# Weight tiles ahead of x in the set-up, a reordered start of the second phase, one image summed by TensorE, and the last chunk finished in thirds

## What is computed

```python
def _attn_kernel(x, w1, b1, w2, b2, bn_gamma, bn_beta, bn_mean, bn_var):
    k = lax.conv_general_dilated(x, w1, (1, 1), padding=[(PAD, PAD), (PAD, PAD)], rhs_dilation=(DIL, DIL), ...)
    k = jax.nn.relu(k + b1[None, :, None, None])          # 128 channels, 7x7, dilation 2
    k = lax.conv_general_dilated(k, w2, (1, 1), 'VALID', ...) + b2[None, :, None, None]   # 49 taps
    ...                                                   # batch norm, relu
    return jax.nn.softmax(k, axis=1)
x = x + conv_ref(_ln_c(x))        # conv_ref: sum over 49 taps of shifted x * attention[tap]
t = _to_tokens(x)
# ffn(_ln_t(t)): one routing per batch element from the mean over its tokens, top 2 of 8 experts,
# gelu(x @ W1 + b1) @ W2 + b2 weighted by the routing, + x, layer norm with gamma and beta
t = t + ffn(_ln_t(t), ...)
```

## Time and profile before

| | us |
|---|---|
| median of 3 runs | 1017.62 |
| lowest and highest of them | 1015.72, 1018.93 |
| profiled execution, its time | 1019.93 |
| profiled execution, its span | 1018.1 |
| TensorE busy (matrix products) | 928.7 |
| VectorE busy | 733.8 |
| ScalarE busy | 544.9 |
| GpSimd busy | 146.2 |

### The profile page before, as it was taken

One profiled execution on the slowest core, in us unless ns is written; L12 is line 12 of the kernel. 1 busy time (PEld: TensorE's weight loads), 2 busy tenths in 40 slices (PEclk: granted clock), 3 DMA queues, 4 the chain that ended last, 5 costly groups with the idle time before them and its releaser, 6 DMA issues. The chain is left out here.

```text
span 1018.1 us, 18938 instructions
## 1 busy us (share of the span) xinstructions
PE 928.7 (91%) x7375; PEld 708.9 (70%) x7375; DVE 733.8 (72%) x1820; ACT 544.9 (54%) x985; POOL 146.2 (14%) x163
## 2 busy tenths in 40 slices
PE   2678999999999999979999925999999999999997
PEld 1567666776677667646999913777777777777776
DVE  4776456559637844977579864778987897888876
ACT  5677333435443512223555435768768686686851
POOL 1100001000100011100213220111111121112111
PEclk9999999999999999989999967999999999999999
DMA  9722121004101104453458444273345435424311
GB/s 234 192 76 65 31 63 47 25 1 131 52 24 27 59 28 137 149 168 86 123 157 229 122 128 97 60 174 79 63 102 135 93 74 140 108 55 95 63 33 47
DMA packets 135080, 96.02 MB, mean 94 GB/s; under 512 B 63579, under 2 KB 129516, under 8 KB 134892
## 3 DMA queue, kind: packets, MB, share of 16 engines
q1 hardware_dynamic: 134990, 94.81, 36.5%
HBM read 55.95 MB, written 29.40 MB: 84 GB/s over the span
## 5 line engine op out<-in xcount | busy, mean ns | idle before, releaser
L1279 PE MATMUL pM<-V,U 128*128 128x368 f16 (+3 forms) x2016 | 321.0, 315 | 0.0
L1279 PEld LDWEIGHTS pM<-V,U 128*128 128x128 f16 x2016 | 194.9, 98 | 101.6 <-issue 0.8
L2047 PE MATMUL pH<-xT,w1h 128*128 128x384 f16 x768 | 190.7, 331 | 15.2 <-DMA xT<-xs 12.8
L1945 DVE SCALAR_TENSOR_TENSOR gl<-gf,sc,gh 128x384 f16<-128x384 f32 x192 | 145.2, 791 | 58.0 <-ACT gh L1761 57.9
L1770 ACT ACTIVATE gf<-pH,b1c,sc 128x384 f32<-128x384 f32 x192 | 127.7, 669 | 97.8 <-issue 72.8
L2063 PE MATMUL pY<-w2h,gh 128*128 128x256 f16 x576 | 157.0, 273 | 0.0
L2063 PE MATMUL pY<-w2h,gl 128*128 128x256 f16 x576 | 157.0, 273 | 0.0
L2063 PE MATMUL pY<-w2l,gh 128*128 128x256 f16 x576 | 157.0, 273 | 0.0
L744 ACT CAST V<-pV 128x384 f16<-128x384 f32 x96 | 45.5, 477 | 155.9 <-PE pV L1250 155.8
L2047 PE MATMUL pH<-xT,w1l 128*128 128x384 f16 x384 | 126.9, 331 | 0.0
L2047 PEld LDWEIGHTS pH<-xT,w1h 128*128 128x128 f16 x768 | 75.7, 99 | 65.3 <-DMA xT<-xs 12.9
(11 more groups left out here) (251 smaller groups left out, 1321.7 us busy)
## 6 DMA issues: line engine op xcount, KB each, us to landing
xa<-in_xt SPq DMA_DIRECT2D x16, 576.0 KB, 6.5
xs_scratch<-xs SPq DMA_DIRECT2D x16, 576.0 KB, 3.9
tk<-t_scratch SPq DMA_DIRECT2D x24, 384.0 KB, 3.9
out<-o SPq DMA_DIRECT2D x24, 384.0 KB, 2.9
xs<-in_ew SPq DMA_DIRECT2D x16, 512.0 KB, 4.8
U<-xs_scratch SPq DMA_DIRECT2D x16, 480.0 KB, 4.7
w1r<-in_ew SPq DMA_DIRECT2D x8, 512.0 KB, 4.3
w2r<-in_ew SPq DMA_DIRECT2D x8, 512.0 KB, 5.8
```

Of the source, the lines that this page charges most:

```text
L1279: return nc.tensor.matmul(out[:, :, first:end], U[:, k, hi_u, piece, :], V[:, b % 2, hi_v, k, c, :, first + TILES * d:end + TILES * d], st ...
L1945: stt(gl[:, sl, j, :], gf[:, (JB * m + j) % GBUFS, :], scale_of(G_UP), gh[:, sl, j, :], ALU.mult, ALU.subtract).then_inc(g_step, 1)
L2047: last = nc.tensor.matmul(pH[:, (JB * m + j) % HBUFS, 0:CN], w[:, k, c, f * P:(f + 1) * P], xT[:, s, x, c, :], start=(i == 0), stop=(i == ...
```

## The change

It has four parts.

1. **Set-up.** SyncE issues ident, w0 and w1 first, then x0, Gt, Td, x1, the small parameters, x2 and w2 to w7. The data turns of image p lie in pair p, at steps 1 to 6, so image 0's are no longer ahead of pair 0, and pair 3 has six. `x_high`, `x_low` and the normalising of image p + 1 lie in pair p. VectorE runs `spread_mags(0)`, `ln(0)`, `tap_scale(0)`, `ln(1)` ahead of pair 0. The batch-norm steps move to steps 2 and 4 of pair 0.
2. **Image 14.** TensorE sums its tokens (`sum_tokens(14)`) behind the last `attend`; VectorE doesn't accumulate it. The means get one more small reduction.
3. **Start of the second phase.** SyncE waits for the routing right behind the loads of chunks 0 and 1, and issues w1, b1, the transpose of chunk 0, w2, b2, chunk 2, the transpose of chunk 1, beta, gamma, chunk 3, the transpose of chunk 2. ScalarE's and VectorE's `take_x(0, 0)` come earlier, `split_w1(0)` comes ahead of `take_x(0, 1)`, GpSimd's first `add_beta` waits for the split of w1, and b2's sum is a step of its own (`sum_b2`) placed later. `layer1` takes the four products with w1's high half first and waits for the low half only in front of the fifth.
4. **Last chunk.** `finish_last` does sum, statistics, power, scale and end for one tile of 128 tokens after the other, and `store_last` stores each tile by itself.

```diff
@@ -227,9 +227,10 @@
     U_PAIR = PIECES // 2
-    MAGS_FIRST, MAGS_THEN = (1, 4), (1, 3)
+    MAGS_THEN = (1, 3)
+    V_LATE = U_PAIR - V_TURNS
     LN_PARTS, NORM_PARTS = {1: 0, 2: 1, 3: 2}, {0: 0, 2: 1, 4: 2}
-    XHI_AT, SPREAD_AT, BN_AT, LN_BACK_AT = 5, 4, 2, 5
+    XHI_AT, SPREAD_AT, BN_AT, LN_BACK_AT = 5, 4, 4, 5
     XBUFS = 3
@@ -568,20 +569,20 @@
-            load_x(0)
-            sp.dma_start(Td[:, :, :], data_d).then_inc(tab_loaded, 16)
-            load_x(1)
-            sp.dma_start(Gt[:, :], tap_d).then_inc(tap_loaded, 16)
             sp.dma_start(ident[:, :], ident_d).then_inc(id_loaded, 16)
...
                 load_w(sp, g)
-            load_x(2)
-            for g in range(2, OGS):
-                load_w(sp, g)
+            load_x(0)
+            sp.dma_start(Gt[:, :], tap_d).then_inc(tap_loaded, 16)
+            sp.dma_start(Td[:, :, :], data_d).then_inc(tab_loaded, 16)
+            load_x(1)
             sp.dma_start(w2s, w2).then_inc(par_loaded, 16)
...
             sp.dma_start(b1s[:, :], b1).then_inc(par_loaded, 16)
+            load_x(2)
+            for g in range(2, OGS):
+                load_w(sp, g)
             for i in range(BI):
@@ -813,25 +814,22 @@
+            for g in range(2):
+                magnitude(g)
             normalise_x(0)
-            x_high(0)
-            normalise_x(1)
-            for j in range(V_TURNS):
-                v_high(j)
-                if j in MAGS_FIRST:
-                    magnitude(MAGS_FIRST.index(j))
-            x_high(1)
             for pair in range(PAIRS_OG):
...
                     u_high(U_PAIR * pair + j)
-                    if j < V_TURNS and pair + 1 < BI:
-                        v_high(V_TURNS * (pair + 1) + j)
+                    if pair + j == 0:
+                        x_high(0)
+                    if j >= V_LATE:
+                        v_high(V_TURNS * pair + j - V_LATE)
                     if j in MAGS_THEN and pair + 1 < PAIRS_OG:
                         magnitude(2 * (pair + 1) + MAGS_THEN.index(j))
-                    if j in NORM_PARTS and pair + 2 <= BI:
-                        normalise_x(pair + 2, third(NORM_PARTS[j]))
-                    if j == XHI_AT and pair + 2 <= BI:
-                        x_high(pair + 2)
+                    if j in NORM_PARTS:
+                        normalise_x(pair + 1, third(NORM_PARTS[j]))
+                    if j == XHI_AT:
+                        x_high(pair + 1)
@@ -1030,10 +1028,13 @@
+            def added(n):
+                return n - ADDED * BI - (n > BY_PE)
+
             def accumulate(n):
...
                 b, i = n // BI, n % BI
-                s = Steps(dve, acc_step, n - ADDED * BI, NB)
+                s = Steps(dve, acc_step, added(n), NB)
                 s.settle()
@@ -1114,40 +1115,34 @@
+            spread_mags(0)
             ln(0)
+            tap_scale(0)
             ln(1)
-            x_low(0)
-            for j in range(V_TURNS):
-                v_low(j)
-                if j in (1, 3):
-                    ln_stats(2, third(j // 2))
-            spread_mags(0)
-            tap_scale(0)
-            x_low(1)
-            ln(2, third(2))
             for pair in range(PAIRS_OG):
...
                     u_low(U_PAIR * pair + j)
-                    if j < V_TURNS and pair + 1 < BI:
-                        v_low(V_TURNS * (pair + 1) + j)
-                    if j in LN_PARTS and pair + 3 <= BI:
+                    if pair + j == 0:
+                        x_low(0)
+                    if j >= V_LATE:
+                        v_low(V_TURNS * pair + j - V_LATE)
+                    if j in LN_PARTS and pair + 2 <= BI:
                         if LN_PARTS[j] < 2:
-                            ln_stats(pair + 3, third(LN_PARTS[j]))
+                            ln_stats(pair + 2, third(LN_PARTS[j]))
                         else:
-                            ln(pair + 3, third(2))
+                            ln(pair + 2, third(2))
                     if j == SPREAD_AT and pair + 1 < PAIRS_OG:
                         spread_mags(pair + 1)
-                    if pair == 0 and j == 0:
+                    if pair == 0 and j == 2:
                         dve.wait_ge(par_loaded, 16 * 7)
...
                         bn_scales()
-                if pair + 2 <= BI:
-                    x_low(pair + 2)
+                x_low(pair + 1)
@@ -1205,8 +1200,6 @@
                     normalise(B - 1, n - 1)
-                if n == IMGS - 1:
-                    accumulate(n - 1)
                 statistics(n)
@@ -1220,21 +1213,22 @@
             means = mean[:, :].rearrange("p (c b) -> p c b", c=CC)
-            dve.wait_ge(tokens_summed, ADDED * BI + B - ADDED)
+            dve.wait_ge(tokens_summed, ADDED * BI + B - ADDED + 1)
             dve.wait_ge(shifts_summed, B)
...
             nc.vector.tensor_reduce(means[:, :, 0:ADDED], summed[:, :, 0:ADDED], AX.X, ALU.add).then_inc(mean_step, 1)
-            nc.vector.tensor_copy(means[:, :, ADDED:B], summed[:, :, ADDED:B, 0]).then_inc(mean_step, 1)
+            nc.vector.tensor_copy(means[:, :, ADDED:B - 1], summed[:, :, ADDED:B - 1, 0]).then_inc(mean_step, 1)
+            nc.vector.tensor_reduce(means[:, :, B - 1], summed[:, :, B - 1, 0:BI:BY_PE % BI], AX.X, ALU.add).then_inc(mean_step, 1)
             nc.vector.tensor_reduce(shifts, pC[:, SHIFTS:SHIFTS + NB * IMGS].rearrange("p (b x) -> p b x", b=B),
...
             nc.vector.tensor_copy(wsum[:, :], pC[:, SUMS_AT:SUMS_AT + UNITS]).then_inc(wsum_taken, 1)
...
@@ -1337,16 +1331,15 @@
-            pe.wait_ge(tab_loaded, 16)
             pe.wait_ge(set_up, POOL_SET)
-            for j in range(V_TURNS):
-                turn_v(j)
             bound(0)
...
                     turn_u(U_PAIR * pair + j)
-                    if j < V_TURNS and pair + 1 < BI:
-                        turn_v(V_TURNS * (pair + 1) + j)
+                    if pair == 0 and j == V_LATE:
+                        pe.wait_ge(tab_loaded, 16)
+                    if j >= V_LATE:
+                        turn_v(V_TURNS * pair + j - V_LATE)
                     if j == U_PAIR - 2 and pair + 1 < PAIRS_OG:
@@ -1499,6 +1492,7 @@
                     sum_shifts(n // BI - 1)
+            sum_tokens(BY_PE)
             turn_stats(B - 1)
@@ -1645,6 +1642,12 @@
+            def store_last():
+                n = B * CHUNKS - 1
+                for t in range(CT):
+                    sp.wait_ge(end_step, E_ALL * (t + 1))
+                    sp.dma_start(out[ds(n * CN + t * P, P), :], o[:, n % 2, t]).then_inc(out_stored[n % 2], 16)
+
             def load_experts(b):
@@ -1657,6 +1660,8 @@
                     sp.dma_start(b1r[:, k], ew_b(eb1, e)).then_inc(b1_loaded, 16)
+                if is_first(b):
+                    turn_x(0, 0)
                 for k, e in enumerate(chosen):
@@ -1668,13 +1673,15 @@
                 load_chunk(0, m)
+            sp.wait_ge(r_step, 16)
+            load_experts(0)
+            load_chunk(0, 2)
+            turn_x(0, 1)
             sp.dma_start(bet[:, :], beta.broadcast_to([P, C])).then_inc(gb_loaded, 16)
             sp.dma_start(gam[:, :], gamma.broadcast_to([P, C])).then_inc(gb_loaded, 16)
-            sp.wait_ge(r_step, 16)
-            load_experts(0)
-            for m in range(2, AHEAD):
+            for m in range(3, AHEAD):
                 load_chunk(0, m)
-            for m in range(XAHEAD):
+            for m in range(2, XAHEAD):
                 turn_x(0, m)
@@ -1687,10 +1694,13 @@
                         turn_x(*later(b, m, XAHEAD, CHUNKS))
-                    store_chunk(b, m)
+                    if later(b, m, 1, CHUNKS):
+                        store_chunk(b, m)
+                    else:
+                        store_last()
@@ -1714,14 +1724,19 @@
             pool.wait_ge(gb_loaded, 32)
+            pool.wait_ge(w1_step, TOPK)
             add_beta(0, 0)
...
                         add_beta(*later(b, m, 1, CHUNKS))
-                    rsqrt(b, m)
+                    if later(b, m, 1, CHUNKS):
+                        rsqrt(b, m)
             batch_loop(body)
+            for t in range(CT):
+                pool.wait_ge(end_step, E_ALL * t + E_VE)
+                nc.gpsimd.tensor_tensor(rstd[:, t:t + 1], ve[:, t:t + 1], mhalf[:, t:t + 1], ALU.pow).then_inc(end_rstd, 1)
@@ -1788,13 +1803,13 @@
             normalise(0, 0)
+            take_x(0, 0)
             act.wait_ge(r_step, 17)
...
             nc.scalar.activation(rc[:, 7:8], rc[:, 4:5], ACT.Gelu)
-            take_x(0, 0)
             normalise(0, 1)
+            split_w1(0)
             take_x(0, 1)
-            split_w1(0)
             act.wait_ge(bias_step, 1)
@@ -1910,6 +1925,9 @@
                         s.did(nc.vector.tensor_copy(b1c[:, :, :], b1r[:, :, :]))
+
+            def sum_b2(b):
+                s = Steps(dve, bias_step, b, 3, 1)
                 dve.wait_ge(b2_loaded, 32 * (b + 1))
@@ -1990,11 +2008,36 @@
+            def finish_last():
+
```

(37 more changed lines are left out.)

17 lines of the change are left out of this document (10 added, 7 removed).

## The result

| | before | changed |
|---|---|---|
| median of the runs | 1017.73 us | 1002.94 us (998.96 to 1005.72) |
| ratio to before, 95% interval | 1 | 0.9844 [0.9807, 0.9881] |
| profiled execution: time, span | 1019.93, 1018.1 us | 1000.76, 999.0 us |
| predicted | | 998.7 us, range 993 to 1006 |

The change takes 1.6% off. The forecast was 998.7 us: direction and range hold, and the gain is smaller by 4 us in the medians. The span that the sum gave, 999.2 us, was met almost exactly by the profiled execution (999.0), in part by luck, as is shown further down.

What follows compares the result with a forecast made beforehand. TensorE was taken to bound the body, leaving gains only at set-up, handover and tail. Terms 8.4 + 2.0 + 7.5 + 1.0 = 18.9 us off gave span 999.2, median 998.7 us; range 993 to 1006.

Steps and rivals of the forecast that it cites:

- Set-up, -8.4 forecast: Before the convolution: new load and work order puts its first turn at 95.7 instead of 104.15 us; bounds -14 and -1.
- Rival (a): Set-up: the start gives half, as one pair at 1.2 GHz costs about 6.5 us more; 1005 us, chance 0.18.
- The prediction's sign of being wrong: Set-up: TensorE's clock below 1.00 in two pairs, listed among the signs that would show the forecast wrong.
- Image 14, -2.0 forecast: End of first phase: VectorE no longer adds image 14's tokens, 2.06 us; ten TensorE column products fall into idle time.
- Handover, -7.5 forecast: Start of second phase: earlier first transpose lets layer 1 begin at about 611.9 instead of 619.45 us; bounds -4.5, -8.7.
- `add_beta` now runs beside VectorE's split of x: Second phase's start: GpSimd's addition moves from x's first split to its second; counted as nothing.
- The pause ahead of layer 2: Chunk 0 of the second phase: a pause not there before would show the forecast wrong; no size given.
- which I take to be later: nothing: Chunk 0's layer 2 waits for the b2 sum, 0.9 us at most, but also for chunk 1's layer 1, taken as later.
- Tail, -1.0 forecast: Behind the last product: ending and storing the last chunk tile by tile saves 1.0 us; bounds -1.7 and +0.9.
- forecast 0.5 + 0.45 us: Tail: last tile ends at 1014.6 instead of 1015.13 us (0.5); last store takes 2.5 instead of 2.95 us (0.45).
- The Trainium skill's fixed part of about 2 us: Last store: a DMA costs about 2 us fixed plus a part by size, so an estimated 2.3 us for 128 KB.
- taking the difference of one profiled execution off a median: Whole kernel: differences of the profiled span, 1018.1 us, were taken off the runs' median, 1017.62 us, giving 998.7 us.

Runs made afterwards that it cites:

- the tail alone: The kernel before with only the last chunk ended and stored in thirds, and the b2 sum moved ahead; 1017.94 us, ratio 1.0017.
- the second trace of the changed kernel: The changed kernel measured and profiled once more, with no edit; 1000.28 us, ratio 0.9835, span 998.6 us.
- the run with the interleaved end: The changed kernel with the steps of the last chunk's three tiles interleaved; 1000.33 us, ratio 0.9848.
- without the collision: The changed kernel with beta and gamma loaded ahead of the routing's wait and GpSimd's first add_beta right behind x's first low part; 1000.10 us, ratio 0.9841.
- image 14 alone: The kernel before with only the 15th image's tokens summed by TensorE instead of VectorE; 1015.31 us, ratio 0.9977.
- image 4 within pair 3: The changed kernel with image 4's normalising, high part and low part moved to earlier steps of pair 3; 998.31 us, ratio 0.9810.
- all five edits: The changed kernel with image 4 earlier, add_beta behind w1's split, w2's split ahead of x's third, interleaved end, third chunk loaded and normalised earlier; 997.09 us, ratio 0.9783.

## Why the prediction was right, and where it was off

**Set-up, -8.4 forecast.** The chain of loads, magnitudes, `ln(0)` and `tap_scale` was right to 0.3 us (17.34 for 17.1, first V turn 24.68 for 24.4), and pair 1 began 0.9 us early (40.27 for 41.2). Pair 1 lasted 18.1 us for 18.3; pair 2, for which I went halfway to an old pair with low clock (19.4), lasted 16.8; pair 3 lasted 17.7 for 16.8. The turn came at 92.92 for 95.7. What the sum left out is a low clock at the convolution's start, 2.5 us. The sum took the stretch behind the turn as unchanged. That it lies 2.8 us below the sum at the turn and 2.5 above behind it cancels, which is luck: -8.55 at the mark. The low clock may have to do with the idle 4.38 us that image 4's split now makes, but that isn't shown: the tail alone has it behind 1.88 us (5.82 us for the 21 products), and shortening the wait to 2.26 us didn't remove it (4.4 to 5.0 us in three traces).
Rival (a), a low clock in pair 0, came in a part of the traces. In this one pair 0 is granted 1.00 and pair 1 0.91, at no cost against its forecast. In the second trace of the changed kernel the low stretch is in pair 0 (0.93), and the turn is at 92.82, so it cost nothing. In the run with the interleaved end, whose set-up is the same, there is one in pair 0 and one in pair 1, and the turn was 3.0 us later. The prediction's sign of being wrong, a clock below 1.00 in two pairs, is there too (pairs 1 and 3, 0.91 and 0.95), and yet the gain came.

**Image 14, -2.0 forecast:** -2.2. There are twenty column products, not ten; they end at 580.7 us, ahead of `accumulate(15)`, so it makes no difference.

**Handover, -7.5 forecast:** -7.2, the transpose landing 5.0 us after its issue for the 4.7 taken. The step that failed is "`add_beta` now runs beside VectorE's split of x": a wait for the weights' split was added, but gamma's load, moved behind the second transpose on SyncE, was later still. I followed GpSimd's added wait and not the moved load, though both are in the diff.
The pause ahead of layer 2, which the prediction had named as a sign of being wrong, is 1.41 us, but the collision's share of it is small: VectorE starts x's third split at 617.06 us, 0.4 us behind ScalarE's part of it (615.75 + 0.94), and without the collision layer 2 came 0.36 us earlier against layer 1. The larger part of the pause is a term that the prediction had put at nothing, `sum_b2` ahead of w2's split ("which I take to be later: nothing"). It measured 0.8 us (the 0.34 and 0.48 us at 618.00) and lies on the way to `b2z`: from the third split to w2's split it is 618.77 - 617.06 = 1.71 us, in the trace of image 14 alone, with the old start, 634.12 - 633.17 = 0.95. There TensorE ran at full clock behind the 2.36 us wait, waited 0.30 us for `b2z`, and layer 2 started 20.81 us behind layer 1. Against that the new start is 1.4 us slower. It did not show in the sum, since in the trace of the kernel before there was a low clock at the same place: layer 2 started 22.55 us behind layer 1 there and 22.23 after. So it is luck that nothing was lost between the two traces. No run moves `sum_b2` alone.

**Tail, -1.0 forecast:** -0.9. A third took 2.66 us for 2.55 (the power of one column on 128 rows is 0.73, between the bounds taken), so the last `o` row is only 0.1 us nearer to the last product; the rest is the last store. From the end of the last `o` row to the end of the span it is 999.0 - 996.79 = 2.2 us, for 2.95 before and the 2.5 taken; from issue to landing the 128 KB stores take 1.7 us. So of the forecast 0.5 + 0.45 us the first came as 0.1 and the second as 0.75: the sum is near by luck.
The Trainium skill's fixed part of about 2 us ("DMA: Bandwidth & Descriptors", Anatomy of one DMA) gave an estimated 2.3 us; the measured 1.7 us is below even the fixed part, and the measurement decides. That section gives its figure for transfers that GpSimd issues, and these stores go out on SyncE's queue.

**The median.** The span's difference, 19.1 us, is the forecast's 18.9. The medians differ by 14.8 us in the first measurement and by 15.9 in the second (1016.16 and 1000.28). The step that failed is taking the difference of one profiled execution off a median: that execution was at 1019.93, 2.3 us above the median of its runs, the one after at 1000.76, 2.2 below. The two had different mean granted clocks, 0.968 before and 0.973 after. Over all executions the time goes with it: beside the second measurement the kernel before took 1015.2 to 1016.1 us in its five executions at 0.973 and 1019.5 to 1023.7 in the three at 0.965 to 0.968. The changed kernel took 999.0 to 1000.8 in its four at 0.973 and 1003.7 to 1005.7 in the three at 0.966 to 0.968. Like with like the gain is thus some 16 us. What makes it less than the 19.1 us of the two spans, and where the low stretches of the untraced executions lie, isn't shown. From the turn ahead of the convolution to image 14's columns the work is the same in the changed kernel and its variants, and the traces need 483.5 (image 4 within pair 3) to 487.9 us (all five edits), so the convolution alone varies by 4.4 us between traces, which is more than the gap. That is the likely place, but it is not proved. The same holds for the tail alone, whose gain of 0.8 us is in its rows and not in its median.

## What to carry to other kernels

A stretch at low clock can stand at the start of a dense stretch (here 2.5 us, behind a wait of 4.38 us, and 3.0 us in another trace, behind one of 1.88): count it too, ask of a gain in one trace whether such a stretch has only moved, and expect that a gain which removes a wait beside one isn't seen. Where a change moves a load, follow the load to every engine that waits for it, and see beside what the released work will then run: VectorE's operations with two inputs in SBUF took 1.5 to 3.2 us longer beside a pair of GpSimd additions. And when a step is put ahead of others in a queue, as the b2 sum was ahead of w2's split, add it to the chain of whatever waits for them. An edit of under 0.3% is read from rows counted from a common event, not from the time.

## What the runs showed of the hardware that I had not expected

- At the second chunk's layer 1, behind the same wait of 2.35 or 2.36 us, the same program ran on at full clock in one trace (0.82 us for four products) and at half clock in the other (1.46 us). At the convolution's start it was low behind 4.38 us in every trace (4.7 to 5.6 us for 21 products instead of 3.34), low for a shorter or equal time behind 2.26 us (4.4 and 5.0 us), and behind the 1.88 us of the old set-up full in three traces and low in one (5.82 us).
- The first 16 products of U's turns take 2.93 and 2.77 us for eight, about twice the later 1.49, though the clock column stands at 1.00 in that stretch. What holds them there isn't known.
- A VectorE operation on a single column lasts 1.78 us when a GpSimd addition over 768 columns is ahead of it; the GpSimd pair itself takes 3.57 to 4.25 us in all of these places.
- GpSimd's power costs 0.55 us for one column on 49 rows, 0.73 for one column on 128 rows. For three columns the median of 24 in the kernel before is 0.86 us, the longest 1.83; the 1.02 of the earlier trace rows is not the usual one.
- SyncE's issue of one transpose lasted between 1.31 and 5.04 us in the changed kernel (median 1.44), and one landed 3.6 to 8.0 us after its issue.
